# Heads to output experts in a decoder layer: first masked output in the last pair, first output sums ahead of the last exponential sums, experts fetched in parts

## Reference

```
gates  = sigmoid(x @ w_gate)                      # 8 heads x 8 experts
gm     = one_hot(argmax(gates)) * gates           # one expert per token and head
values = einsum('bhne,ehdk,bnd->bhnk', gm, value_experts, x)
attn   = softmax(mask(q * scale @ k))             # causal, 8 heads of 64
out    = einsum('bhij,bhjk->bhik', attn, values)
out    = einsum('bhne,ehkd,bhnk->bhnd', gm, output_experts, out).sum(heads)
x      = x + out
```

## Time and profile before

| | |
|---|---|
| median of 3 runs | 969.93 us (967.42 to 970.67) |
| profiled execution | 971.46 us, of which 969.7 span from the first to the last instruction |
| mean granted TensorE clock | 0.984 |
| busy: TensorE, its weight loads | 911.0 us (94%), 678.0 us (70%) |
| busy: VectorE, ScalarE, GpSimd | 616.9 (64%), 308.0 (32%), 315.7 us (33%) |

### The profile page before, as it was taken

One profiled execution on the slowest core, in us unless ns is written; L12 is line 12 of the kernel. 1 busy time (PEld: TensorE's weight loads), 2 busy tenths in 40 slices (PEclk: granted clock), 3 DMA queues, 4 the chain that ended last, 5 costly groups with the idle time before them and its releaser, 6 DMA issues.

```text
span 969.7 us, 15805 instructions
## 1 busy us (share of the span) xinstructions
PE 911.0 (94%) x6316; PEld 678.0 (70%) x6316; DVE 616.9 (64%) x932; ACT 308.0 (32%) x494; POOL 315.7 (33%) x309
## 2 busy tenths in 40 slices
PE   6989899999989989799999998999999989988998
PEld 3668678877744544699976786887775445448998
DVE  5758566567454564778868575765664454558887
ACT  4535555100245445101033355630003334440000
POOL 5112321211584677316610032300013553761000
PEclk9999999999999999889999999999999999989999
DMA  8112000444053453255530000021221010024653
GB/s 269 49 33 100 1 1 8 130 130 130 1 159 105 153 186 99 70 165 180 179 127 1 2 1 1 2 71 67 87 87 44 1 25 1 24 68 133 194 179 125
DMA packets 40959, 82.16 MB, mean 85 GB/s; under 512 B 12407, under 2 KB 17751, under 8 KB 40887
## 3 DMA queue, kind: packets, MB, share of 16 engines
q1 hardware_dynamic: 40887, 81.16, 26.6%
HBM read 61.65 MB, written 19.33 MB: 84 GB/s over the span
## 4 chain that ended last, share of the span: by engine, by line
PE 84%; DVE 8%; DMA 3%; issue 2%; ACT 1%; POOL 1%; SPq 1%; POOLq 0%; DVEq 0%
PE ps L1172 18%; PE ps L1539 11%; PE ps L1471 6%; DVE region L1027 5%; PE ps L1545 5%; PE ps L1391 5%; PE ps L1443 5%; PE ps L1345 5%; PE ps L1180 4%; PE ps L1412 4%; PE ps L1297 3%; PE ps L1359 3%; PE ps L1312 2%; PE ps L1485 2%; PE ps L1214 2%
## 5 line engine op out<-in xcount | busy, mean ns | idle before, releaser
L584 POOL TENSOR_TENSOR xT<-xT,region 128x1024 f32<-128x1024 f32 (+5 forms) x80 | 130.6, 1632 | 99.8 <-PE ps L1471 72.3
L1539 PE MATMUL ps<-expert_hi,k_hi 128*128 128x256 f32 x512 | 130.5, 291 | 9.4 <-DVE k_hi L1117 6.8
L1027 DVE TENSOR_REDUCE region<-ps 128x2 f32<-128x1024 f32 (+2 forms) x96 | 91.7, 956 | 60.0 <-PE ps L1418 36.6
L1539 PE MATMUL ps<-expert_lo,k_hi 128*128 128x256 f32 x512 | 128.8, 288 | 0.0
L1081 DVE COPY_PREDICATED region<-region,ps 128x512 f32<-128x512 uint32 x112 | 82.3, 735 | 72.0 <-PE ps L1172 71.5
L1539 PEld LDWEIGHTS ps<-expert_hi,k_hi 128*128 128x128 f32 x512 | 100.4, 196 | 13.4 <-DVE k_hi L1117 7.2
L1172 PE MATMUL ps<-expert_hi,wide_hi 128*128 128x512 f32 x256 | 103.9, 406 | 0.0
L1539 PEld LDWEIGHTS ps<-expert_lo,k_hi 128*128 128x128 f32 x512 | 101.3, 198 | 0.0
L1117 DVE TENSOR_TENSOR k_hi<-region 128x1024 fp32r<-128x1024 f32 x64 | 82.9, 1296 | 27.2 <-PE ps L1545 26.8
L1172 PE MATMUL ps<-expert_hi,wide_lo 128*128 128x512 f32 x256 | 100.0, 391 | 0.0
L1172 PE MATMUL ps<-expert_lo,wide_hi 128*128 128x512 f32 x256 | 99.9, 390 | 0.0
(11 more groups left out here) (157 smaller groups left out, 1721.1 us busy)
## 6 DMA issues: line engine op xcount, KB each, us to landing
region<-hot_rows SPq DMA_DIRECT2D x128, 128.0 KB, 3.7
expert_hi<-halves_kept SPq DMA_DIRECT2D x24, 512.0 KB, 3.8
expert_lo<-halves_kept SPq DMA_DIRECT2D x24, 512.0 KB, 5.1
halves_kept<-expert_hi SPq DMA_DIRECT2D x16, 512.0 KB, 5.3
halves_kept<-expert_lo SPq DMA_DIRECT2D x16, 512.0 KB, 6.1
expert<-in_value_experts SPq DMA_DIRECT2D x8, 512.0 KB, 4.5
expert<-in_output_experts SPq DMA_DIRECT2D x8, 512.0 KB, 4.4
gb<-scale_rows SPq DMA_DIRECT2D x16, 256.0 KB, 3.9
```

Source lines behind the costliest of these rows:

```text
L584: pool.tensor_tensor(acc(c)[:, heads, lo:CH], acc(c)[:, heads, lo:CH], PT[:, k % RING, heads, lo:CH], ALU.add).then_inc(sem["added"], 1)
L1027: dve.tensor_reduce(mx[:, :, at:at + 1], ps[:, 6:8, 0:w], AX.X, ALU.max).then_inc(sem["s_max"], 1)
L1539: mm(ps[:, 4 + t // 2, t % 2 * D:(t % 2 + 1) * D], k_hi[n % 2][:, t * P:(t + 1) * P], w[:, slot, columns], start=(n == 0 and t % 2 == 0 an ...
```

## The change

- **Order of steps.** (1,2) comes ahead of (0,3). `normalise(3)` moves from behind the masks of step 3 to behind those of step 5.
- **First masked output.** Its high operation is made on VectorE in block 5 of pair 3 and its low one in block 6; `masked` is split in two functions. In pair 3, `scaled(2)` moves from block 5 to block 4 and `normalise(2)` from block 10 to block 9.
- **Start of the output sums.** Behind the last `weigh`, TensorE runs the high matmuls of step 0 for six of the eight tiles, then `sums(3, 1)`, which now writes bank 0, then the other two tiles and the low matmuls.
- **Roundings.** `rounded(4)` and `(5)` come behind ScalarE's last exponential, `outputs_low(4)` and `(5)` behind GpSimd's last addition.
- **Masks.** The first four are fetched ahead of pair 2's sums, the fifth ahead of pair 3's sums, the sixth and seventh between pair 3's sums and scales.
- **Experts.** A fetch is split in two parts with semaphores of their own: the columns of pairs 0 to 2 (asked for once step (e,2) is done) and those of pair 3 (once (e,3) is done), so four transfers where there were two. In the first batch the output experts are made in the order 2 to 7, 0, 1, so that 0 and 1 lie in the slots when the outputs begin and are not fetched back.

```diff
@@ -58,9 +58,9 @@
-    SUMMED = [(0, 0), (0, 1), (0, 2), (1, 0), (1, 1), (0, 3), (1, 2), (1, 3)]
+    SUMMED = [(0, 0), (0, 1), (0, 2), (1, 0), (1, 1), (1, 2), (0, 3), (1, 3)]
     SUMMED += [(e, p) for e in range(2, E3) for p in range(PAIRS3)]
-    LAST_OF = {e: max(n for n, (x, _) in enumerate(SUMMED) if x == e) for e in range(E3)}
+    STEP_OF = {at: n for n, at in enumerate(SUMMED)}
     GW = G + H3
...
@@ -247,13 +247,16 @@
+        ORDER = [*range(E3), *range(E3 + SLOTS, PIECES), *range(E3, E3 + SLOTS)]
         PIECES_AT = {(0, 2): 8, (0, 5): 9, (0, 8): 10, (1, 2): 11, (1, 5): 12, (1, 8): 13, (2, 2): 14, (2, 6): 15}
         PARTS = [(p, c) for p in range(PAIRS3) for c in range(NC)]
-        ROUND_AT = {(2, 7): 0, (2, 9): 1, (3, 2): 2, (3, 3): 3, (3, 10): 4, (3, 11): 5}
-
-
-        SCALED_AFTER, NORMALISED_AFTER = 2, 3
+        ROUND_AT = {(2, 7): 0, (2, 9): 1, (3, 2): 2, (3, 3): 3}
+        SCALED_AFTER, NORMALISED_AFTER = 2, 5
+        MASKS_AHEAD = SCALED_AFTER + 1
+        MASKED_AT = {5: 0, 6: 1}
+
@@ -288,23 +291,28 @@
+        def sums_bank(p, c):
+
+            return 0 if (p, c) == (PAIRS3 - 1, NC - 1) else 6
+
...
-        def piece_used(eng, b, q):
+        def piece_used(eng, b, q, p=PAIRS3 - 1):
...
             else:
-                until(eng, "mo_used", b, LAST_OF[q - E3] + 1)
-
-        def piece_here(eng, b, q):
-
-            if b == 0 and q < E3:
-                until(eng, "piece_lo", 0, q + 1)
+                until(eng, "mo_used", b, STEP_OF[q - E3, p] + 1)
+
+        def piece_here(eng, b, q, last):
+
+            if b == 0 and q < E3 + SLOTS:
+                until(eng, "piece_lo", 0, ORDER.index(q) + 1)
             else:
-                eng.wait_ge(piece_in[q % SLOTS], 32 * ((b * PIECES + q - E3) // SLOTS + 1))
+                fetched = 32 * ((b * PIECES + q - E3 - SLOTS) // SLOTS + 1)
+                eng.wait_ge((last_in if last else piece_in)[q % SLOTS], fetched)
@@ -349,11 +357,17 @@
-            def fetch_piece(b, q):
-
+            def fetch_piece(b, q, last):
+
+                cs = slice((PAIRS3 - 1) * D, PAIRS3 * D) if last else slice(0, (PAIRS3 - 1) * D)
                 for half, w in enumerate((expert_hi, expert_lo)):
-                    sp.dma_start(w[:, q % SLOTS, :].bitcast(fp32), halves_kept[q, half]
-                                 ).then_inc(piece_in[q % SLOTS], 16)
+                    sp.dma_start(w[:, q % SLOTS, cs].bitcast(fp32), halves_kept[q, half, :, cs]
+                                 ).then_inc((last_in if last else piece_in)[q % SLOTS], 16)
+
+            def fetch_whole(b, q):
+
+                for last in (False, True):
+                    fetch_piece(b, q, last)
@@ -364,19 +378,20 @@
-            def load_piece(q):
-
+            def load_piece(k):
+
+                q = ORDER[k]
                 sp.dma_start(expert[:, :], d["value_experts" if q < E3 else "output_experts"][:, q % E3, :]
...
-            def keep_piece(q):
-
-                until(sp, "piece_lo", 0, q + 1)
-                if q + 1 < PIECES:
-                    load_piece(q + 1)
+            def keep_piece(k):
+
+                until(sp, "piece_lo", 0, k + 1)
+                if k + 1 < PIECES:
+                    load_piece(k + 1)
                 for half, w in enumerate((expert_hi, expert_lo)):
-                    sp.dma_start(halves_kept[q, half], w[:, q % SLOTS, :].bitcast(fp32)
-                                 ).then_inc(piece_kept[q % SLOTS], 16)
+                    sp.dma_start(halves_kept[ORDER[k], half], w[:, k % SLOTS, :].bitcast(fp32)
+                                 ).then_inc(piece_kept[k % SLOTS], 16)
@@ -412,14 +427,18 @@
                         piece_used(sp, b, q - SLOTS)
-                        fetch_piece(b, q)
+                        fetch_whole(b, q)
                         if q == SLOTS:
...
                         piece_used(sp, b, q - SLOTS)
-                        fetch_piece(b, q)
+                        fetch_whole(b, q)
                 for p in range(PAIRS3):
                     split = [PIECES_AT[at] for at in sorted(PIECES_AT) if at[0] == p and b == 0]
+                    if p == PAIRS3 - 1:
+                        until(sp, "v3_ready", b, TT + 1)
+                        for n in range(MASKS):
+                            fetch_mask(b, n)
                     if p:
@@ -428,29 +447,31 @@
                         keep_piece(q)
-                    if b == 0 and p == PAIRS3 - 2:
-                        for i in range(SLOTS):
-                            sp.wait_ge(piece_kept[i], 32 * (PIECES // SLOTS))
-                        for q in range(E3, E3 + SLOTS):
-                            fetch_piece(b, q)
-
-                until(sp, "v3_ready", b, TT + 1)
-                for n in range(MASKS):
-                    fetch_mask(b, n)
+
+                def next_mask(n):
+
+                    until(sp, "mo_lo_ready", b, n + 1)
+                    fetch_mask(b, n + MASKS)
+
+                next_mask(0)
                 spread_sums(b, PAIRS3 - 1)
+                for n in range(1, MASKS_AHEAD):
+                    next_mask(n)
                 spread_scales(b, PAIRS3 - 1)
+                if b == 0:
+                    for i in range(SLOTS):
+                        sp.wait_ge(piece_kept[i], 32 * (PIECES // SLOTS))
                 for n in range(NEP):
-                    if n + MASKS < NEP:
-                        until(sp, "mo_lo_ready", b, n + 1)
-                        fetch_mask(b, n + MASKS)
-                    e = SUMMED[n][0]
-                    if n == LAST_OF[e] and e + SLOTS < E3:
-                        piece_used(sp, b, E3 + e)
-                        fetch_piece(b, E3 + e + SLOTS)
+                    if MASKS_AHEAD <= n < NEP - MASKS:
+                        next_mask(n)
+                    e, p = SUMMED[n]
+                    if p >= PAIRS3 - 2 and e + SLOTS < E3:
+                        piece_used(sp, b, E3 + e, p)
+                        fetch_piece(b, E3 + e + SLOTS, p == PAIRS3 - 1)
                 if b + 1 < B:
...
                         piece_used(sp, b, PIECES - SLOTS + q)
-                        fetch_piece(b + 1, q)
+                        fetch_whole(b + 1, q)
                 for i in range(TC):
...
@@ -816,9 +837,11 @@
                             rounded(ROUND_AT[p, u])
+                for k in range(len(ROUND_AT), NC * (PAIRS3 - 1)):
+                    rounded(k)
                 outputs(PAIRS3 - 1, 1)
                 sums(PAIRS3 - 1, 1)
-                for k in range(len(ROUND_AT), len(PARTS)):
+                for k in range(NC * (PAIRS3 - 1), len(PARTS)):
                     rounded(k)
@@ -1071,6 +1094,24 @@
+
+                def masked_high(n):
+
+                    p, i = SUMMED[n][1], n % 2
+                    dve.wait_ge(mask_in[n % MASKS], 32 * ((b * NEP + n) // MASKS + 1))
+                    if n < 2:
+                        until(dve, "st_ps", b, (PAIRS3 - 1 + n) * NB)
+                    else:
+                        until(dve, "mo_used", b, n - 1)
+                    dve.tensor_tensor(k_hi[i][:, :], oT[:, p, :], masks[:, n % MASKS, :], ALU.mult
+                                      ).then_inc(sem["mo_hi_ready"], 1)
+
+                def masked_low(n):
+
+                    p, i = SUMMED[n][1], n % 2
+                    until(dve, "o_lo_ready", b, NC * (p + 1))
+                    dve.tensor_tensor(q_hi[i][:, :], o_lo(p).bitcast(fp32), masks[:, n % MASKS, :], ALU.mult
+                                      ).then_inc(sem["mo_lo_ready"], 1)
@@ -1101,27 +1142,17 @@
                             add_up(u)
-                        if p and u == 5:
+                        if p and u == (4 if p == PAIRS3 - 1 else 5):
                             scaled(p - 1)
-                        if p and u == ROW_AT:
+                        if p == PAIRS3 - 1 and u in MASKED_AT:
+                            (masked_high, masked_low)[MASKED_AT[u]](0)
+                        if p and u == (ROW_AT - 1 if p == PAIRS3 - 1 else ROW_AT):
                             normalise(p - 1)
-                def masked(n):
-
-                    p, i = SUMMED[n][1], n % 2
-                    dve.wait_ge(mask_in[n % MASKS], 32 * ((b * NEP + n) // MASKS + 1))
-                    if n < 2:
-                        until(dve, "st_ps", b, (PAIRS3 - 1 + n) * NB)
-                    else:
-                        until(dve, "mo_used", b, n - 1)
-                    dve.tensor_tensor(k_hi[i][:, :], oT[:, p, :], masks[:, n % MASKS, :], ALU.mult
-                                      ).then_inc(sem["mo_hi_ready"], 1)
-                    until(dve, "o_lo_ready", b, NC * (p + 1))
-                    dve.tensor_tensor(q_hi[i][:, :], o_lo(p).bitcast(fp32), masks[:, n % MASKS, :], ALU.mult
-                                      ).then_inc(sem["mo_lo_ready"], 1)
-
                 for n in range(NEP):
-                    masked(n)
+                    if n:
+                        masked_high(n)
```

(31 more changed lines are left out.)

## The result

The changed kernel takes 952.16 us (median of 4 runs, 951.19 to 953.32); the kernel before takes 969.6 in the same session (4 runs). The ratio is 0.9824, 95% interval 0.9811 to 0.9837: 17.4 us less, where 20.5 were forecast. The forecast was 949.4 with a range of 945 to 957. The changed kernel's profiled execution took 951.45 (span 948.7), so between profiled executions the difference is 20.0, between spans 21.0.

What follows compares the result with a forecast made beforehand. TensorE bounds the kernel, so only its idle or slow-clock time can be won: 5.03 + 5.81 + 3.0 + 2.1 + 4.6 = 20.5 us, from the median 969.93 to 949.4, range 945 to 957.

Steps and rivals of the forecast that it cites:

- B: Output step 4's wait for its masked output, behind pair 3's normalisation, shrinks: 3.0 and 2.1 us won in the two batches.
- C: Around output step 8, TensorE's waits for expert 2's fetch go in both batches: 3.60 + 1.04 = 4.6 us won.
- A: At the start of the output stage, TensorE's waits for the last exponential and addition go: 5.03 and 5.81 us won.
- rival 2: Pair 3 pays for the masks: GpSimd's additions delayed, TensorE waits, last sums late; 6.9 us less won, 956.3; chance 0.07.
- Rival 1: Step 4's stall only moves to step 6: scales' write queues 4.2 us, 962.6, chance 0.05; half of it 956, 0.09.
- Rivals 3 and 4: 3: masks late in every expert, 978, chance 0.03; 4: no change, time won returns before second batch, 969, chance 0.03.

Runs made afterwards that it cites:

- the scales sooner: The changed kernel with one mask pair, not two, fetched between pair 3's sums and its scales; 950.77 us, ratio 0.9812.

## Why the prediction was right, and where it was off

**Mechanism.** Right in B and C: the waits named are gone, and the old order and the whole fetch bring them back. In A the waits went too, but not by the edit that they were put down to (below). Pieces of 0.23, 1.56 and 0.56 stand at steps 6 and 7 of the first batch where 0.55, 1.7 and 0.9 were forecast, the middle one for the low mask, through GpSimd.

**A, mis-sized by 1.2.** The term was: 4.04 us from the weight sums to step 0, no wait at the sums. It is 4.66, and the 0.62 between them is the wait: the sums start 0.74 behind the last of the twelve matmuls, and such matmuls start 0.12 apart. (The bracket says 0.47, since it counts from that matmul's end.) The cause is that VectorE's last two additions take 1.99 beside GpSimd's 3.80 us of roundings where I put two of at most 0.69 from the earlier trace rows; they end 2.93 behind the start of the weight sums, where 2.1 was forecast. The same crowding shows in pair 3: 2.30 for a masked output, where it takes 1.21 alone, and 1.77 for an addition. By the rule of the Trainium skill that the prediction weighed (SBUF — State Buffer, section "Who interferes with whom") such instructions of the two engines exclude each other. The trace agrees, 2.30 against 1.21. GpSimd's additions were not delayed enough to reach TensorE, which has no wait in pair 3. So rival 2 fell but for these 0.62 in each batch.

**A's cause, half wrong.** The prediction put A's waits down to the roundings' order. The roundings put back cost nothing; the first mask made in pair 3 is worth 5.9. And part of A was no gain of its own: of the 1.4 us that the twelve matmuls ahead of the sums bring at step 0 of each batch, step 6 takes back about half, and with the old order (A and C alone) only 9.3 of the 18.75 are left. The first mask (a part of A), the order and the split fetch, taken back one at a time, cost 5.9, 9.5 and 6.4, together 21.8, more than the 18.75 that the whole change won. So the parts don't add up singly. The prediction's sum came out near because it priced B with A already in place (it had TensorE at 390.02 there) and C behind both.

**B.** Forecast 5.1, measured 4.88, in part by luck. Two errors cancelled in part in the arrival of the scales: counted from the weight sums, VectorE got to the reciprocal 0.7 sooner (one of step 1's two operations ran beside GpSimd, not both), and the scales' write took 2.9, not 1.6. The prediction took no queueing because 256 KB of masks stood in front; there were 512 KB, and with 256 KB (the scales sooner) the write took 1.9 and 1.6. Rival 1 is that write: it did queue, for a third of the 4.2 that it was given. In the second batch the loss is 3.68 where 3.05 was forecast, though the only wait is 1.57: behind it the clock fell, as this window shows. Which batch it falls in is not the change's: in the other profile of this kernel it was the first.

```profile
873.80:877.70 3.90, 3.90 (x22) 3.90 (x21) 2.73 (x3) 0.00 (x0) 0.00 (x0) 0.57 0.71 195
```

**C.** 4.6 forecast; 3.60 in the first batch, as forecast, 0.67 for 1.04 in the second, where the fallen clock reaches into it.

**Rivals 3 and 4** fell: behind step 9 no step waits for a mask, and the second batch moved up with the first. The earlier mask fetches and the two experts that are not fetched back were not taken back singly; that they are worth nothing is argued, not shown.

**Time.** 952.16 against 949.4. Of the 2.8 us, 1.75 is missing in the stretch (18.75 of 20.5). The rest, about 1, lies outside the stretch. In the other profile of the changed kernel the clock fell in both front stages, as it did before the change; against that profile before, the spans differ by 17.8 and the stretches by 18.4, so 0.6 is lost again, nearly all of it ahead of the first stretch (which begins at 386.52, before at 385.98). What this is, and how the clock fell in the runs that were only timed, is not shown.

## What to carry to other kernels

Where a chain through other engines and DRAM ends at a fixed step, starting the work ahead of it earlier mostly lengthens the wait there: find the last link of each chain (here the last addition, then the write of the scales, then an expert's transfer) and move the consumer or the link, not the idle matmuls. Take the parts of an edit back one at a time and compare the sum of the losses with the joint gain: if it is larger, the parts depend on each other. Compare stretches of single profiles only at equal granted clock. In one queue, what is moved ahead of something makes that something late; price the transfer passed as well as the one that passes.

## What was not expected of the hardware

- A write of 8 KB took 1.6 us with no mask fetch ahead of it in the stage, 1.6 to 1.9 behind one pair (256 KB) and 2.4 to 2.9 behind two pairs in the same queue (the changed kernel and those experiments that keep both pairs there).
- Steps of the output stage take 2.83 us in some stretches and 2.80 in others at granted clock 1.00, in the same run: in the first batch of the changed kernel, 2.83 from step 0 to 5 and 2.80 from step 7 on. The cause is open.
- The granted clock fell in the front stages, and behind step 6's wait, in some executions and not in others of the same kernel; it cost 1.57 to 1.60 us in the windows of the front stages and 1.5 to 1.8 in a stretch.
